# Middle stage of a graph layer: the gate of the alpha_l gathers is split off, and VectorE's arithmetic from variance to expert choice is rewritten with two instructions fewer

## The reference, cut to what matters

```python
xn = layernorm(x)                                     # x is 12500 x 256
# graph part: one edge per node (row i of the edge list), 4 heads of 64
xt = (xn @ weight).reshape(-1, 4, 64)
alpha = softmax(leaky_relu(alpha_l[src] + alpha_r[dst], 0.01), axis=1)
tmp = einsum('nh,nhd->nd', alpha[:n], xt[dst[:n]])    # repeated for each head
# linear attention over all 12500 rows: q, k = elu(.) + 1, context = k^T v, 1/D, Wproj
x = x + gnn + mix
# feed-forward with 8 experts, capacity 1954 rows each
h = layernorm(x)
logits = h @ gate_w + gate_b
probs = softmax(logits); idx = argmax(probs)          # first of equals
pos = running count of rows with the same expert      # rows beyond the capacity are dropped
y = (relu(h @ w1[idx] + b1[idx]) @ w2[idx] + b2[idx]) * probs[idx]
x = x + y
```

## Time and profile before

| | us |
|---|---|
| median of 3 runs | 1488.85 (1488.57 to 1491.13) |
| the profiled execution, its own time | 1488.98 |
| its span in the trace | 1487.1 |
| busy in the span: TensorE, VectorE, ScalarE, GpSimd | 1390.6, 1130.4, 906.1, 690.7 |

### The profile page before, as it was taken

How to read it: one execution, slowest core, us unless ns; L and a number is a source line. 1 busy time by engine, 2 the same in 40 slices (tenths; PEclk the granted TensorE clock), 3 DMA queues, 4 the chain that set the end, 5 groups by cost and what they waited for, 6 DMA issues and landing times.

```text
span 1487.1 us, 30487 instructions
## 1 busy us (share of the span) xinstructions
PE 1390.6 (94%) x9008; PEld 1245.1 (84%) x9008; DVE 1130.4 (76%) x2919; ACT 906.1 (61%) x2045; POOL 690.7 (46%) x604
## 2 busy tenths in 40 slices
PE   6999999998989889887599999999999999999995
PEld 5999999997777777776399999999999999999995
DVE  6888888884698888898556867678677776777765
ACT  3545554553376666676467667676676766757663
POOL 1211001112788878875506454464554544545534
PEclk9999999998799999999699999999999999999998
DMA  4444334432444544456111211223122231212001
GB/s 99 79 89 78 86 74 89 88 76 67 96 121 119 127 126 126 118 129 183 41 58 47 68 29 25 81 50 96 41 58 66 53 91 41 76 41 52 7 15 20
DMA packets 131134, 112.46 MB, mean 76 GB/s; under 512 B 69068, under 2 KB 116877, under 8 KB 130936
## 3 DMA queue, kind: packets, MB, share of 16 engines
q1 hardware_dynamic: 78196, 72.83, 19.7%
q0 software_dynamic: 52864, 38.82, 11.8%
HBM read 76.17 MB, written 43.85 MB: 81 GB/s over the span
## 4 chain that ended last, share of the span: by engine, by line
PE 50%; issue 0%; DVE 0%; POOL 0%; POOLq 0%; ACT 0%; DVEq 0%; ACTq 0%
PE psY L1767 24%; PE psH L1790 24%; PE psX L1741 2%; POOL out L1482 0%; POOLq L1289 0%; ACT q_all L1537 0%; DVE q_all L1717 0%; DVE q_all L1728 0%; DVE q_all L1730 0%; DVE q_all L1666 0%; DVE q_all L1723 0%; DVE fin L1719 0%; DVE q_all L1715 0%; POOLq L1482 0%; DVEq L35 0%
## 5 line engine op out<-in xcount | busy, mean ns | idle before, releaser
L1684 DVE TENSOR_TENSOR h_lo<-q_all,h_hi 128x496 fp32r<-128x496 f32 x256 | 173.0, 676 | 197.6 <-PE psY L1767 87.0
L1463 POOL DMA_INDIRECT out<-q_all,to_i x124 | 173.5, 1399 | 311.5 <-issue 286.7
L1551 ACT ACTIVATE h_hi<-psH,b_sb 128x496 fp32r<-128x496 f32 x256 | 172.4, 673 | 232.1 <-PE psH L1790 222.3
L1767 PE MATMUL psY<-w_hi,h_hi 128*124 128x256 f32 x1024 | 289.2, 282 | 0.0
L1767 PE MATMUL psY<-w_hi,h_lo 128*124 128x256 f32 x1024 | 287.1, 280 | 0.0
L1767 PE MATMUL psY<-w_lo,h_hi 128*124 128x256 f32 x1024 | 286.8, 280 | 0.0
L1767 PEld LDWEIGHTS psY<-w_lo,h_hi 128*124 128x124 f32 x1024 | 188.9, 184 | 8.9
L1767 PEld LDWEIGHTS psY<-w_hi,h_hi 128*124 128x124 f32 x1024 | 188.8, 184 | 8.0
L1767 PEld LDWEIGHTS psY<-w_hi,h_lo 128*124 128x124 f32 x1024 | 189.1, 185 | 0.0
L1446 POOL DMA_INDIRECT q_all<-out,from_i x112 | 163.5, 1460 | 54.6 <-issue 54.6
L1553 ACT ACTIVATE q_all<-psH,b_sb 128x496 f32<-128x496 f32 x256 | 170.7, 667 | 0.0
(11 more groups left out here) (257 smaller groups left out, 3215.3 us busy)
## 6 DMA issues: line engine op xcount, KB each, us to landing
x_sb<-in_x SPq DMA_DIRECT2D x50, 448.0 KB
q_all<-in_L_ffn_w SPq DMA_DIRECT2D x16, 1024.0 KB, 7.4
graph_table<-tab_sb SPq DMA_DIRECT2D x25, 511.0 KB
out<-xd SPq DMA_DIRECT2D x25, 448.0 KB
x_sb<-in_x SPq DMA_DIRECT2D x50, 52.0 KB
out<-q_all,to_i POOLq DMA_INDIRECT x128, 4.3
q_all<-out,from_i POOLq DMA_INDIRECT x112, 4.7
graph_table<-tab_sb SPq DMA_DIRECT2D x25, 59.3 KB
```

What stands on the lines that cost most here:

```text
L1463: pool.indirect_dma_start(out=out, in_=o_sb[:, par, j, :], in_offset=None, out_offset=bass.IndirectOffsetOnAxis(ap=to_i[:, par, j:j + 1], ...
L1551: act.activation(h_hi[:, f % 4, :], psH[f % 2][:, 0:TS3], ACT.Relu, bias=b1_sb[:, bass.ds(e * NF + f, 1)]).then_inc(s_hhi_ready, 1)
L1684: nc.vector.tensor_tensor(h_lo[:, f % 4, :], hf[:, f % 4, :], h_hi[:, f % 4, :].bitcast(F32), ALU.subtract).then_inc(s_hlo_ready, 1)
L1767: ins = nc.tensor.matmul(psY[par][j // 2][0:T3, (j % 2) * D:(j % 2 + 1) * D], hh[:, f % 4, j * T3:(j + 1) * T3], w[:, f, :], start=f == 0 ...
```

## The change

Two edits in the middle stage. First, GpSimd's `gather` becomes `gather_left` (the four `gl`) and `gather_rows` (the four `gx`). `gather_left` for step s + 2 now waits for `s_att` (L992 of step s, the last reader of `gl`), `gather_rows` still for `s_pr`. Second, VectorE's arithmetic: the Newton step for the reciprocal root is written as (near - 3) * std, with the factor -0.5 moved into the product with the logits; and in the choice `lex` is computed first, and the mask is made from it in one instruction (lex == 0) * desc. The exponentials of the logits get a buffer of their own, `lexp`.

```diff
-            NATT, NPR, NLG, NROUTE, NPLACE, NAWAY = 7, 3, 3, 11, 4, 9
+            NATT, NPR, NLG, NROUTE, NPLACE, NAWAY = 7, 3, 3, 10, 4, 9
...
                 def step(s, par, h, ahead):
                     if ahead > 1:
-                        pool.wait_ge(s_pr, NPR * s + 1)
+                        pool.wait_ge(s_att, NATT * s + 1)
                         pool.wait_ge(idx_in[par], 16 * (h + 1))
                         passed(pool, s_pool_passed)
-                        gather(par, idx[:, par, :, :])
+                        gather_left(par, idx[:, par, :, :])
+                        pool.wait_ge(s_pr, NPR * s + 1)
+                        passed(pool, s_pool_passed)
+                        gather_rows(par, idx[:, par, :, :])
...
-                    act.activation(lex[:, :, :], lex[:, :, :], ACT.Exp).then_inc(s_l_exp, 1)
+                    act.activation(lexp[:, :, :], lex[:, :, :], ACT.Exp).then_inc(s_l_exp, 1)
...
-                    nc.vector.tensor_scalar(near[:, :], near[:, :], -0.5, 1.5, ALU.mult, ALU.add).then_inc(s_rstd2, 1)
-                    dve.wait_ge(s_rstd2, 4 * s + 3)
-                    nc.vector.tensor_tensor(rstd[:, :], near[:, :], std[:, :], ALU.mult).then_inc(s_rstd2, 1)
-                    dve.wait_ge(s_rstd2, 4 * s + 4)
+                    nc.vector.scalar_tensor_tensor(rstd[:, :], near[:, :], 3.0, std[:, :], ALU.subtract, ALU.mult)\
+                      .then_inc(s_rstd2, 1)
+                    dve.wait_ge(s_rstd2, 3 * s + 3)
                     dve.wait_ge(s_lg, NLG * s + 1)
-                    nc.vector.tensor_tensor(lg[:, :, :], lg[:, :, :], wide(rstd[:, :], E), ALU.mult).then_inc(s_lg, 1)
+                    nc.vector.scalar_tensor_tensor(lg[:, :, :], lg[:, :, :], -0.5, wide(rstd[:, :], E),
+                                                   ALU.mult, ALU.mult).then_inc(s_lg, 1)
...
                     dve.wait_ge(s_route, NROUTE * s + 1)
-                    nc.vector.tensor_tensor(eqm[:, :, :], lg[:, :, :], wide(lmax[:, :], E), ALU.is_equal).then_inc(s_route, 1)
                     nc.vector.tensor_tensor(lex[:, :, :], lg[:, :, :], wide(lmax[:, :], E), ALU.subtract).then_inc(s_route, 1)
                     dve.wait_ge(s_route, NROUTE * s + 2)
-                    nc.vector.tensor_tensor(eqm[:, :, :], eqm[:, :, :], desc[:, :, :], ALU.mult).then_inc(s_route, 1)
+                    nc.vector.scalar_tensor_tensor(eqm[:, :, :], lex[:, :, :], 0.0, desc[:, :, :], ALU.is_equal, ALU.mult)\
+                      .then_inc(s_route, 1)
...
-                    nc.vector.tensor_reduce(lsum[:, :], lex[:, :, :], axis=AX.X, op=ALU.add).then_inc(s_route, 1)
+                    nc.vector.tensor_reduce(lsum[:, :], lexp[:, :, :], axis=AX.X, op=ALU.add).then_inc(s_route, 1)
```

More of the change, by code:

```diff
@@ L686, in gps_layer @@
             lex = sb2("lex", [T, J, E])
+            lexp = sb2("lexp", [T, J, E])
             lsum = sb2("lsum", [T, J])
@@ L820, in _, with gather_left, gather_rows @@
             def _(pool):
[L821 to L826, removed]
+                def gather_left(par, at):
+                    for j in range(J):
+                        pool.indirect_dma_start(out=gl[:, par, j, :], out_offset=None, in_=table_l,
+                                                in_offset=bass.IndirectOffsetOnAxis(ap=at[:, 0, j:j + 1], axis=0))\
+                            .then_inc(gat[par], 16)
+                def gather_rows(par, at):
+                    for j in range(J):
+                        pool.indirect_dma_start(out=gx[:, par, j, :], out_offset=None, in_=table,
+                                                in_offset=bass.IndirectOffsetOnAxis(ap=at[:, 1, j:j + 1], axis=0))\
+                            .then_inc(gat[par], 16)
                 for s in range(2):
-                    gather(s, idx_all[:, s, :, :])
+                    gather_left(s, idx_all[:, s, :, :])
+                    gather_rows(s, idx_all[:, s, :, :])
                 def step(s, par, h, ahead):
                     if ahead > 1:
-                        pool.wait_ge(s_pr, NPR * s + 1)
+                        pool.wait_ge(s_att, NATT * s + 1)
                         pool.wait_ge(idx_in[par], 16 * (h + 1))
                         passed(pool, s_pool_passed)
-                        gather(par, idx[:, par, :, :])
+                        gather_left(par, idx[:, par, :, :])
+                        pool.wait_ge(s_pr, NPR * s + 1)
+                        passed(pool, s_pool_passed)
+                        gather_rows(par, idx[:, par, :, :])
                 over_steps(pool, step)
@@ L888, in root @@
                     act.wait_ge(s_aggr2, J * (s + 1))
-                    act.wait_ge(s_rstd2, 4 * s)
+                    act.wait_ge(s_rstd2, 3 * s)
                     act.activation(std[:, :], mv[:, :, 1], ACT.Ln, bias=eps2[:, :]).then_inc(s_ln, 1)
@@ L894, in logit_exp @@
                 def logit_exp(s):
-                    act.wait_ge(s_route, NROUTE * s + 3)
-                    act.activation(lex[:, :, :], lex[:, :, :], ACT.Exp).then_inc(s_l_exp, 1)
+                    act.wait_ge(s_route, NROUTE * s + 2)
+                    act.activation(lexp[:, :, :], lex[:, :, :], ACT.Exp).then_inc(s_l_exp, 1)
                 def one_hots(s):
@@ L1062, in choose @@
                     dve.wait_ge(s_route, NROUTE * s + 1)
-                    nc.vector.tensor_tensor(eqm[:, :, :], lg[:, :, :], wide(lmax[:, :], E), ALU.is_equal).then_inc(s_route, 1)
                     nc.vector.tensor_tensor(lex[:, :, :], lg[:, :, :], wide(lmax[:, :], E), ALU.subtract).then_inc(s_route, 1)
                     dve.wait_ge(s_route, NROUTE * s + 2)
-                    nc.vector.tensor_tensor(eqm[:, :, :], eqm[:, :, :], desc[:, :, :], ALU.mult).then_inc(s_route, 1)
+                    nc.vector.scalar_tensor_tensor(eqm[:, :, :], lex[:, :, :], 0.0, desc[:, :, :], ALU.is_equal, ALU.mult)\
+                      .then_inc(s_route, 1)
+                    dve.wait_ge(s_route, NROUTE * s + 3)
+                    nc.vector.tensor_reduce(wmax[:, :], eqm[:, :, :], axis=AX.X, op=ALU.max).then_inc(s_route, 1)
                     dve.wait_ge(s_route, NROUTE * s + 4)
-                    nc.vector.tensor_reduce(wmax[:, :], eqm[:, :, :], axis=AX.X, op=ALU.max).then_inc(s_route, 1)
+                    nc.vector.tensor_tensor(oh[:, :, :], eqm[:, :, :], wide(wmax[:, :], E), ALU.is_equal).then_inc(s_route, 1)
                     dve.wait_ge(s_route, NROUTE * s + 5)
-                    nc.vector.tensor_tensor(oh[:, :, :], eqm[:, :, :], wide(wmax[:, :], E), ALU.is_equal).then_inc(s_route, 1)
-                    dve.wait_ge(s_route, NROUTE * s + 6)
                     with nc.allow_low_precision("sums of at most four ones"):
@@ L1080, in place @@
                     nc.vector.tensor_tensor(seen[:, :], seen[:, :], oh_sum[:, :], ALU.add).then_inc(s_route, 1)
-                    dve.wait_ge(s_route, NROUTE * s + 8)
+                    dve.wait_ge(s_route, NROUTE * s + 7)
                     nc.vector.tensor_reduce(slotf[:, :], picked[:, :, :], axis=AX.X, op=ALU.add).then_inc(s_route, 1)
-                    dve.wait_ge(s_route, NROUTE * s + 10)
+                    dve.wait_ge(s_route, NROUTE * s + 9)
                     dve.wait_ge(s_at_ready, 3 * J * s)
@@ L1087, in place @@
                     dve.wait_ge(s_l_exp, s + 1)
-                    nc.vector.tensor_reduce(lsum[:, :], lex[:, :, :], axis=AX.X, op=ALU.add).then_inc(s_route, 1)
+                    nc.vector.tensor_reduce(lsum[:, :], lexp[:, :, :], axis=AX.X, op=ALU.add).then_inc(s_route, 1)
                     dve.wait_ge(s_place, NPLACE * s + 1)
                     nc.vector.tensor_scalar(blk[:, :], blk[:, :], ROUND, ROUND, ALU.add, ALU.subtract).then_inc(s_place, 1)
-                    dve.wait_ge(s_route, NROUTE * s + 11)
+                    dve.wait_ge(s_route, NROUTE * s + 10)
                     nc.vector.reciprocal(prb[:, :], lsum[:, :]).then_inc(s_place, 1)
@@ L1161, in q_ksum @@
                     if not (isinstance(s, int) and s < 4):
-                        pe.wait_ge(s_route, NROUTE * (s - 4) + 8)
+                        pe.wait_ge(s_route, NROUTE * (s - 4) + 7)
                     n = 0
@@ L1230, in positions @@
                 def positions(s, ahead):
-                    pe.wait_ge(s_route, NROUTE * s + 7)
+                    pe.wait_ge(s_route, NROUTE * s + 6)
                     pe.wait_ge(s_inv_t, KC * (s + 3 if ahead > 1 else NS))
```

4 lines of the change are left out of this document (2 added, 2 removed).

## The result

The changed kernel takes 1479.6 us (median of 4 runs, 1477.0 to 1483.9) against 1488.7 of the kernel before: ratio 0.9931 [0.9914, 0.9947]. The kernel before scatters too: in three later batches, of 17 to 23 executions each, its medians are 1490.2 to 1490.7 and single executions range from 1487.2 to 1497.0.

A forecast was written before the change was run, and what follows sets the result against it. VectorE's own chain was taken to bound the middle stage, about 13.1 us a step. Root 6.9 cut to 5.9 by TensorE, plus 0.4, less 0.2 to 0.6, gave 5.9 us saved: 1483.0 us, range 1480.5 to 1487.6.

The forecast's parts named there:

- Gate 0: GpSimd's gathers in the middle stage: no reader waits for them, so the earlier start saves 0 in the loop.
- the second `gl`: With the new gate GpSimd is up to two gathers ahead; `pr` then holds this gather instead of the last `gx`.
- Root chain -0.33 us a step: VectorE's rstd chain L1044 to L1054, four instructions to three: loses 0.20 pitch plus 0.13 holding a step.
- Choice 0: VectorE's L1061 to L1070: one instruction less saves 0, first instruction to `wmax` staying 0.45 us; bounds 0 and 0.11 a step.
- TensorE takes back 1.0 of 6.9: At the positions (L1235), waiting for `inv_t` limits the gain: 21 x 0.33 = 6.9 us becomes 5.9.
- TensorE's clock adds to both ... about 1 us either way: Three loop steps, 0.7 to 1.5 us longer at lower granted clock, may come or go, widening both bounds.
- Nothing else can move: Only the middle stage (376 to 715 us) changes; the expert stage behind it has no edit.
- the 5.9: Total saving forecast: 5.9 us from the loop, plus 0.4 for two steps, less 0.2 to 0.6 near the end.
- B: Stage end: GpSimd's earlier memset holds VectorE's L1090, costing 3.4 us; 1486.4 us, chance 0.25.
- C: TensorE already bounds the middle stage; only steps with L1049 held gain, 2 to 3 us; 1486.3 us, chance 0.13.
- D: Slower: port stall moves from L1049 onto L1090, 0.39 us a step, plus the memset's 3.4; 1495.0 us, chance 0.07.
- E: The gate does more than credited by mending late gathers; nothing to mend, time as forecast; no chance given.

The follow-up runs named there:

- its work in another order: Root-only kernel with TensorE's denominators and the transpose for `inv_t` issued ahead of older one-hot products: 1483.3 us, 0.9955 of the kernel before; 0.9868 in the low-clock batch.
- one spare instruction: Root-only kernel plus one unused tensor_tensor behind L1046, waited for but read by nobody: 1487.7 us, 0.9977 of the kernel before.
- the memset in the middle: Changed kernel with GpSimd's memset moved between second and third `gx` of the last set: one execution, 1536.5 us in the low-clock batch, no ratio read.
- the unheld four: Kernel before with L1049 as a three-operand instruction no gather holds, still four root instructions: 0.9991 in the low-clock batch; repeated 1491.9 us, 1.0001.

## Why the prediction was right in its mechanism and wrong in its size

- **Gate 0: right.** 1.0003 alone, and no difference with and without it. Of the reasoning, "the second `gl`" was wrong: after the first long step GpSimd is one gather ahead. The held one still ends 1.1 us behind the large product.
- **Root chain -0.33 us a step: mis-sized.** The median of the segment L1044 to L1054 fell from 0.92 to 0.58, but its mean from 0.97 to 0.58, 0.39. The hold and the pitch are there as forecast (with the instruction kept but unheld: 0.78). The rest is a pause of about 0.1 us before L1054 in every second step, which went with the instruction. That is 22 x 0.06 = 1.3 us more than the term had.
- **Choice 0: right.** 1.0010 alone. The rule of the Trainium skill (VectorE: DVE Perf Modes, Rules for kernel authors), to minimise the count of operations, would have given 2.4 us more; the trace does not agree for this instruction, which ran while the next one would have had to wait.
- **TensorE takes back 1.0 of 6.9: too much.** With the root alone the clean step fell by 0.37 of the chain's 0.39: 0.4 us in 21 steps is missing, not 1.0. In the changed kernel it fell by 0.28 and 0.33 in two traces; 0.06 of what is missing there is the longer `mvb` of root and choice together. That TensorE still holds part of a step is shown by its work in another order, which gave 0.15.
- **The step that failed: "TensorE's clock adds to both ... about 1 us either way".** The steps that fall to half clock were sized too small. The three long steps of the kernel before cost 3.1 us over clean ones. The changed kernel has 2 in its profiled execution, the slowest of four, and 1 and 0 in the traces of the same kernel again and of the arithmetic alone. Root alone has none in three traces: of its 10.8 us in the steps 21 x 0.37 = 7.7 is the chain and 3.1 the long ones. With one spare instruction in the same chain the count is 15. Against the kernel before, the long steps were worth from -3.1 to +10.5 us in these traces (15 of them cost 13.6), and the prediction had given them 1 either way.
- **"Nothing else can move": wrong by a little.** The first stage took 1.8 us more and the third 0.6 less in the profiled pair. The former is a stretch of half clock near 20 us that comes and goes with the same code, as the three rows above show; the latter I cannot tell from scatter.
- **Sum.** The profiled pair differs by 5.1 us, near the 5.9; the medians by 9.1. The near 5.1 is luck: it has 1.8 us of the first stage against it, and its execution is 4.3 us above the median. The profile of before is a fair one (1489.0 for 1488.7). The trace of the changed kernel run again (1480.7 us, the median of its batch) divides its 8.3 us like this: clean steps 21 x 0.33 = 6.9, two long steps fewer 1.7, end of stage 0.5, rest 1.0, less 1.8 in the first stage. So against the 5.9 of the forecast it has about 1 us more from the chain and 1.7 from the clock; the executions that make the 9.1 were not profiled one by one.
- **Rivals.** B did not occur, but the memset in the middle shows its price. C is refuted by the clean step, 12.65 to 12.70 us against 12.98, where C would have left it at 13.1 unless L1049 was held. D did not occur: L1100 took 174 ns on average, L1095 225. E: nothing to mend, as said.

Open: what sets at which step length over 3 us at half clock fall into one step. The pauses of about 0.1 us in every second step are open too. Why in one batch the clock was low so much more often cannot be told from these runs. It is not shown to be a property of the chip: that batch (before: 1573.6 us) and the last one (before: 1490.4 us) carry the same chip number.

The best version run is the root part alone: 1477.7, 1477.9 and 1478.3 us in three batches.

## What to carry to other kernels

Count a removed instruction by its pitch (the time from its start to the start of the next) only if the next one really waited for it: here one of two was worth 0.37 us a step and the other nothing, and the order of time in one step told them apart beforehand. Where two engines are nearly level and one of them has its clock granted in stretches, a change of 0.15 to 0.2 us in the step may move the time by more than twice its own sum or not at all: 9.4 us for 4.2 with a spare instruction, nothing for the unheld four. Such a clock belongs into the range with the cost of a long step times the number that could appear, and a lone trace of a variant, whose execution may be the slowest of its batch, does not give the time of its mechanism; spare instructions that change the length alone tell more.

## What the runs showed of the hardware that was not expected

- With a clean step of 12.79 us 15 of 21 steps were long in the profiled execution, the slowest of twelve; with 12.59 and 12.96 us (set by spare instructions alone) none. The time at half clock was 66.0, 32.1 and 32.3 us.
- TensorE can run at half clock for up to 3.00 us of a step without making it long; from 3.07 us on every step was long, in 13 traces.
- In one batch the same kernel ran at 1573.6 us instead of 1490. The trace of the choice alone in that batch has it all in the middle stage: 377.4 us from the second to the last `pr` instead of 301.1, and 770.0 us behind it as elsewhere. A later batch with the same chip number ran at 1490.4.
- In the hardware loop of two steps, 0.1 us before L1054 and 0.07 us in the four `mvb` stand in every second step only; the first is there in every trace in which L1051 is the plain product and in no other, the second with the new choice and the new root together.
